# A four-stage software pipeline of a patch transformer, regrouped: normalization one round ahead, second norm with attention, and one late activation in the last layer

## The reference

```python
x = _fold_to_kernels(in_x)                      # (pixels, 3 tokens, 48)
h = _ln(x); q, k, v = split(h @ w_attn.T)       # 4 heads of 12
att = softmax(einsum('nhtd,nhsd->nhts', q, k) / sqrt(12))
x = x + einsum('nhts,nhsd->nhtd', att, v) @ w_attn_proj.T
h = _ln(x); x = x + gelu(h @ w_fc.T) @ w_fc_proj.T      # 48 -> 192 -> 48
x = _ln(x); out = einsum('bhwc,oc->bohw', sum(x, tokens), conv_w) + conv_b
```

## Time and profile before

| | us |
|---|---|
| median of 3 runs | 11524.5 (11506.01 to 11528.91) |
| the profiled execution | 11512.45 |
| its span | 11510.3 |
| PE busy | 8808.3 (77%) |
| DVE busy | 7862.0 (68%) |
| ACT busy | 7497.3 (65%) |
| POOL busy | 6400.2 (56%) |

### The profile page before, as it was taken

One profiled execution on the slowest core, in us unless ns is written; L12 is line 12 of the kernel. 1 busy time (PEld: TensorE's weight loads), 2 busy tenths in 40 slices (PEclk: granted clock), 3 DMA queues, 4 the chain that ended last, 5 costly groups with the idle time before them and its releaser, 6 DMA issues. The chain is left out here.

```text
span 11510.3 us, 144669 instructions
## 1 busy us (share of the span) xinstructions
PE 8808.3 (77%) x35038; PEld 2895.7 (25%) x35038; DVE 7862.0 (68%) x9543; ACT 7497.3 (65%) x8343; POOL 6400.2 (56%) x3353
## 2 busy tenths in 40 slices
PE   5888888888888888844008888888888888885588
PEld 2333323333333333311002222222222222221133
DVE  5555565555556555643748888888888888886677
ACT  3555555555555555523419889889889988985577
POOL 3444444444444444420008888888888888885111
PEclk8888888888888888877559999999999999998799
DMA  2000000000000000010432322233223322234554
GB/s 74 9 9 7 8 9 9 7 9 9 9 7 9 9 7 9 4 62 29 141 106 60 67 62 59 60 68 65 60 60 67 67 60 60 65 66 91 138 126 117
DMA packets 284359, 562.90 MB, mean 49 GB/s; under 512 B 75120, under 2 KB 205904, under 8 KB 270172
## 3 DMA queue, kind: packets, MB, share of 16 engines
q1 hardware_dynamic: 247858, 536.71, 19.5%
q0 software_dynamic: 35744, 17.87, 0.8%
HBM read 367.98 MB, written 186.07 MB: 48 GB/s over the span
## 5 line engine op out<-in xcount | busy, mean ns | idle before, releaser
L1188 POOL TENSOR_TENSOR l_a<-l_a 128x1018 f32<-128x1018 f32 x2116 | 3920.9, 1883 | 600.4 <-ACT l_a L1349 587.4
L1311 DVE TENSOR_TENSOR l_r<-l_pps,l_a 128x509 f32<-128x509 f32 x4232 | 2642.3, 680 | 651.7 <-PE l_pps L1201 651.6
L1349 ACT ACTIVATE l_a<-l_a 128x2036 f32<-128x2036 f32 x1193 | 2270.1, 1903 | 126.4 <-DVE l_a L1317 100.5
L1201 PE MATMUL l_qps<-l_mv,l_wst 123*128 123x509 bf16 x4246 | 1318.7, 393 | 889.0 <-DMA l_mv<-pw 567.5
L1342 ACT ACTIVATE l_a<-l_qps 128x1018 f32<-128x1018 f32 x1592 | 1591.6, 1019 | 471.9 <-PE l_qps L1201 457.1
L586 POOL TENSOR_TENSOR a_pr<-a_pr 128x768 f32<-128x768 f32 x384 | 877.1, 2284 | 1248.2 <-DVE a_pr L529 1232.4
L540 DVE TENSOR_TENSOR a_x<-a_cps,a_x 128x512 f32<-128x512 f32 x384 | 260.8, 688 | 1624.2 <-PE a_cps L417 1142.8
L665 ACT ACTIVATE a_g<-a_fps 128x512 f32<-128x512 f32 x1152 | 646.0, 595 | 1110.7 <-PE a_fps L410 848.5
L1201 PE MATMUL l_pps<-l_mv,l_wst 123*128 123x509 bf16 x4232 | 1342.9, 389 | 10.9 <-DVE l_r L1311 5.0
L1254 PE MATMUL l_aux<-l_r,l_sums 128*32 128x509 f32 x8448 | 1129.4, 607 | 54.3 <-DVE l_o L1295 33.3
L463 POOL TENSOR_TENSOR a_pr<-a_qkv 128x768 f32<-128x768 f32 x128 | 344.3, 2707 | 1256.5 <-ACT a_qkv L671 1256.5
(11 more groups left out here) (178 smaller groups left out, 11989.3 us busy)
## 6 DMA issues: line engine op xcount, KB each, us to landing
l_mv<-pw SPq DMA_DIRECT2D x1608, 79.5 KB
l_gx<-g SPq DMA_DIRECT2D x66, 1040.0 KB
planes<-l_s SPq DMA_DIRECT2D x67, 1018.0 KB, 4.6
l_sh<-planes SPq DMA_DIRECT2D x536, 127.2 KB, 6.5
a_xt<-g SPq DMA_DIRECT2D x192, 160.0 KB, 3.3
pw<-pw_hi SPq DMA_DIRECT2D x165, 127.2 KB
...
```

The costliest lines, as they stand in the source:

```text
L1188: g.tensor_tensor(a, a, a, ALU.mult).then_inc(sq_p, 1)
L1201: return t.matmul(out, wst[:, k, n * P:(n + 1) * P], x[:, n // NPP, cols], start=True, stop=True)
L1311: v.tensor_tensor(to, pps[:, (2 * m + h) % P_BANKS, 0:SUB], pair_of(A, m)[:, h, :], ALU.mult).then_inc(mul_done, 1)
L1349: s_.activation(a, a, ACT.Abs_reciprocal_sqrt, bias=1.0).then_inc(root_done, GROUP)
```

## The change

In the first layer the steps are regrouped. `STAGE` is now "ahead" (chunk n: centre, var1, `scale_tokens`), "new" (chunk n-1: heads, products, scores, softmax shift and `Exp`), "attn" (chunk n-2: values, mix, project, and now also `square_residual`, `var2` and `scale_residual`), "mlp" (chunk n-3: hidden, gelu, shrink, `add_mlp`, and now also `square_out`, `var3`, `scale_out`, `add_out` and the store). There are still 67 rounds. `Tc` gets a fourth slot, `QKV` a second one, the input `XT` has two slots instead of three. Within a round the groups of the mlp come first, then `project` alternating with `centre` and `var1`, then `var2`, then `var3`. In the last layer each `silu` comes one unit later.

```diff
-TURNS = 3
+TURNS = 4
+SLOTS0 = 2
 BANK = 512
 
-T_GROUPS = {"centre": (3, "new"), "var2": (6, "mlp"), "var1": (3, "new"), "var3": (6, "out"), "mix": (6, "attn")}
+T_GROUPS = {"mix": (6, "attn"), "centre": (3, "ahead"), "var1": (3, "ahead"), "var2": (6, "attn"), "var3": (6, "mlp")}
 C_GROUPS = {"mlp": (6, "mlp"), "proj": (6, "attn")}
-STAGE = {"new": 0, "attn": 1, "mlp": 2, "out": 3}
+STAGE = {"ahead": 0, "new": 1, "attn": 2, "mlp": 3}
+MIX_AT = {3: (0, 1), 4: (2, 3), 5: (4, 5)}
...
+        XT = sb("a_xt", [F2, SLOTS0, TW * H])
         Tc = sb("a_tc", [P, TURNS, TW * H])
...
-        QKV = sb("a_qkv", [P, TW, 3 * F2])
+        QKV = sb("a_qkv", [P, 2, TW, 3 * F2])
...
-                    if n + TURNS < NCHUNKS:
+                    if n + SLOTS0 < NCHUNKS:
                         sp.wait_ge(t_made, p.t_base + p.t_at["centre"] + 3)
-                        load(n + TURNS)
...
-                        pe.wait_ge(h1_made, p.n * 3 + 3)
-                    pe.wait_ge(q_read, p.n * TW + w + 1)
+                        pe.wait_ge(h1_made, p.n * 3)
+                    pe.wait_ge(q_read, (p.n - 1) * TW + w + 1)
...
                 def body(p):
-                    if p.new:
-                        pe.wait_ge(x_in[p.turn], (p.n - p.turn) * 16 + 48)
-                        for g in range(3):
-                            centre(p, g)
-                    if p.mlp:
-                        for g in range(6):
-                            var2(p, g)
-                        hidden(p, 0)
-                    if p.new:
-                        for g in range(3):
-                            var1(p, g)
-                    if p.out:
-                        for g in range(6):
-                            var3(p, g)
                     for g in range(7):
-                        if p.mlp and 0 < g < 6:
+                        if p.mlp and g < 6:
                             hidden(p, g)
                         if p.mlp and g:
                             shrink(p, g - 1)
                         if p.mlp and g < 6:
                             hidden_rest(p, g)
-                        if p.new and 0 < g < 6:
-                            heads(p, 2 * g - 2)
-                            heads(p, 2 * g - 1)
-                        if p.attn and g:
-                            mix(p, g - 1)
+                        if p.new and g < 5:
+                            heads(p, 2 * g)
+                            heads(p, 2 * g + 1)
+                        if p.attn:
+                            for q in MIX_AT.get(g, ()):
+                                mix(p, q)
+                    if p.ahead:
+                        pe.wait_ge(x_in[p.turn % SLOTS0], (p.n - p.turn % SLOTS0) * 24 + 48)
+                    for g in range(6):
+                        if p.attn:
+                            project(p, g)
+                        if p.ahead:
+                            (centre if g < 3 else var1)(p, g % 3)
                     if p.attn:
                         for g in range(6):
-                            project(p, g)
+                            var2(p, g)
+                    if p.mlp:
+                        for g in range(6):
+                            var3(p, g)
...
                     if p.attn:
                         softmax_scale(p)
                         values(p, 0)
                     if p.mlp:
+                        add_mlp(p, 0)
+                    if p.attn:
+                        values(p, 1)
+                    if p.mlp:
+                        add_mlp(p, 1)
+                    if p.attn:
+                        values(p, 2)
+                    if p.mlp:
+                        for g in range(2, 6):
+                            add_mlp(p, g)
+                    for g in range(6):
+                        if p.attn:
+                            add_attention(p, g)
+                        if p.new and g in (1, 2, 3):
+                            products(p, g - 2)
+                    if p.new:
+                        for n in range(5):
+                            score(p, n)
+                        softmax_shift(p)
+                    if p.attn:
                         for g in range(6):
                             scale_residual(p, g)
-                    if p.attn:
-                        values(p, 1)
-                        values(p, 2)
-                    if p.mlp:
-                        for g in range(5):
-                            add_mlp(p, g)
-                    if p.new:
-                        products(p)
-                    if p.mlp:
-                        add_mlp(p, 5)
-                    for g in range(6):
-                        if p.new and g < 5:
-                            score(p, g)
-                        if p.attn:
-                            add_attention(p, g)
-                    if p.new:
-                        softmax_shift(p)
 
                 steps(dve, body)
 
             @block.gpsimd
             def _(pool):
                 g_ = nc.gpsimd
+                pool.sem_inc(z_made, 3)
 
                 def add_values(p, d):
...
 
                 def body(p):
                     if p.attn:
-                        add_values(p, 0)
+                        for d in range(3):
+                            add_values(p, d)
                     if p.new:
+                        pool.wait_ge(q_read, p.n * TW + 2)
+                        if p.attn:
+                            pool.wait_ge(val_p, (p.n - 1) * 6)
+                        for d in (-2, 2):
+                            query_key(g_, p, d).then_inc(sc_p, 1)
+                    if p.ahead:
                         for g in range(3):
                             scale_tokens(p, g)
-                    if p.attn:
-                        add_values(p, 1)
-                        add_values(p, 2)
-                    if p.out:
+                    if p.mlp:
                         for d in range(3):
                             scale_out(p, d)
-                    if p.new:
-                        pool.wait_ge(q_read, p.n * TW + TW + 2)
-                        if p.attn:
-                            pool.wait_ge(val_p, p.n * 6)
-                        for d in (-2, 2):
-                            query_key(g_, d).then_inc(sc_p, 1)
-                    if p.out:
                         add_out(p)
...
                 def read_mix(p, g):
                     s_.activation(yT[:, g, :], made(p, "mix", g)[0:F2, :], ACT.Copy).then_inc(t_read, 1)
 
                 def body(p):
-                    if p.new:
+                    for g in range(6):
+                        if p.mlp:
+                            gelu(p, g)
+                        if p.new and g < 5:
+                            read_heads(p, 2 * g)
+                            read_heads(p, 2 * g + 1)
+                        if p.attn:
+                            for q in MIX_AT.get(g, ()):
+                                read_mix(p, q)
+                        if p.mlp and g in (3, 5):
+                            square_out(p, g // 4)
+                    if p.ahead:
                         for g in range(3):
                             read_centre(p, g)
                     if p.mlp:
+                        square_out(p, 2)
+                    if p.ahead:
+                        for g, (w, n) in enumerate(CENTRE):
+                            inverse_std(p, "var1", g, R1[:, w * H:(w + n) * H])
+                    if p.attn:
                         for d in range(3):
                             square_residual(p, d)
-                    if p.attn:
-                        act.wait_ge(soft, (p.n - 1) * 9 + 6)
-                        s_.activation(At[:], At[:], ACT.Exp, scale=float(HEAD) ** -0.5).then_inc(soft_exp, 1)
-                    if p.mlp:
                         for g in range(6):
                             inverse_std(p, "var2", g, R2[:, g, :])
-                    if p.new:
-                        for g, (w, n) in enumerate(CENTRE):
-                            inverse_std(p, "var1", g, R1[:, w * H:(w + n) * H])
-                    if p.out:
+                    if p.mlp:
                         act.wait_ge(stored, (p.n - 3) * (SETS * 16) + 16)
                         for g in range(6):
                             inverse_std(p, "var3", g, R3[:, g // 2, g % 2 * BANK:(g % 2 + 1) * BANK])
-                    for g in range(7):
-                        if p.mlp and g < 6:
-                            gelu(p, g)
-                        if p.new and 0 < g < 6:
-                            read_heads(p, 2 * g - 2)
-                            read_heads(p, 2 * g - 1)
-                        if p.attn and g:
-                            read_mix(p, g - 1)
-                    if p.mlp:
-                        for d in range(3):
-                            square_out(p, d)
+                    if p.new:
...
             def silu_after(n):
 
```

(2 more changed lines are left out.)

83 lines of the change are left out of this document (41 added, 42 removed).

## The result

| | before | after |
|---|---|---|
| median of 4 runs, us | 11518.5 | 10478.2 (10454.3 to 10487.8) |
| profiled execution, its span, us | 11512.45, 11510.3 | 10485.04, 10483.2 |
| granted clock over the span | 0.877 | 0.922 |

The ratio is 0.909, with a 95% interval of 0.9075 to 0.9113.

The account below looks back on a forecast made before the run. No engine is full, so the order of waits decides. A round of 38.3 + 29.8 = 68.1 us instead of 77.36 saves 565, the last layer 45: 11512.45 - 565 - 45 = 10902.5, median 10915 us, range 10610 to 11290.

Parts of the forecast that it names:

- part B: From the end of the last shrink to the next round's first Gelu: 29.8 us forecast instead of 40.8.
- the clock term: Ahead of var2, TensorE idles about 1.9 us and its clock falls: 1.5 us added, between 0 and 5.
- the first stretch of part A: From a round's first Gelu to the third Gelu of group 1: 11.0 us plus 1.3 for two heads.
- The charge of 1.3 for two heads at half clock: Group 0 gets two heads while TensorE is the slower partner: 1.3 us added, between 0 and 2.
- rival 1: Smaller gain, about 11280 us: GpSimd runs beside VectorE, products cost 6.33 us, half clock follows, round 73.8; chance 0.27.
- the tail: Two mixes and the last shrink, after the third Gelu of group 5: 3.6 us instead of 3.2.
- The first and last rounds: Three rounds at each end of the first layer, same work in other portions: 0 us, bounds 30 either way.
- groups 1 to 4 of part A: Between first Gelu and last shrink: groups 1 and 2 taken as 5.1 us each, groups 3 and 4 as 6.1.
- the three products: VectorE's products, after GpSimd has done its own: 3.2 us for three instead of 6.33.
- the pause of 3.62 us: TensorE waits ahead of hidden_rest(0) for the first Gelu: 3.7 us forecast where there were 2.69.
- the silu: Last layer: one unit later gives loads more time; 45 us saved, up to 105, later gathers possibly losing 20.
- Rival 2: Larger gain, about 10540 us: fewer pauses keep the clock full in early groups and var2, round 61.8; chance 0.10.

Follow-up runs that it names:

- n1: The kernel after, with project, centre and var1 one after the other instead of in turn; 10893.0 us, ratio to before 0.946.
- h1: The kernel after, with each pair of heads one group later (groups 1 to 5 instead of 0 to 4); 10627.4 us, ratio to before 0.922.
- f1: The kernel before, with four unread matmuls of 128 columns in the gap behind hidden_rest(0); 11374.1 us, ratio 0.988.
- h2: h1 with four unread matmuls of 128 columns in the gap behind hidden_rest(0); 10564.8 us, ratio to before 0.917.
- n3: n1 with six unread matmuls of 128 columns in the pause ahead of var2; 10821.2 us, ratio to before 0.939.
- f3: The kernel before, with seven unread matmuls of 128 columns in its pause of 1.77 us ahead of var2; 11516.9 us, ratio 1.000.
- f2: The kernel after, with 14 unread matmuls of 128 columns right behind hidden(0), in the pause before the first Gelu; 10419.9 us, ratio to before 0.9048.

## Why the prediction was wrong

- **The mechanism of part B was right.** A round lost its pauses there, and the engines follow each other as described. From the end of the last shrink (2036.2) the first inverse root starts after 7.9 us, the three squares end after 13.0 (forecast 13.1), the twelve roots after 24.4 (25.0), and the Gelu comes after 27.7, where 28.3 was the sum without the clock term. n1 shows what that order carries: 415 us, of which its own part is 4.7 us a round.
- **The failed step is the first stretch of part A**, "11.0 + 1.3" = 12.3 us. It took 8.6. Three things make up the 3.7 us. The base was wrong by 0.9: 11.0 is the longest of three kinds of round, and the mean was 10.1. The charge of 1.3 for two heads at half clock did not come. And the stretch got 1.5 shorter than before, where the forecast kept the half clock as long as it was, since the pause ahead of it is no shorter. h1, f1 and h2 show that the half clock's length hangs on the small gap behind the pause as well: work put there takes 1.6, 1.6 and 1.2 us off the stretch, even work nobody reads. So the heads were not a cost of 1.3 us but a gain of 1.6. Over 61 full rounds the 3.7 us are 226 us of the 437 missing.
- **The clock term of var2**, 1.5 us, failed next: 92 us. The pause was 1.51 us instead of 1.9, TensorE had run without a gap since 2003.15, and the clock stayed at 1.00 in all 59 rounds. By n3 a fall would have cost 1.4 us in part B, so the size was right and the fall did not come. Why not is shown in part only: in n1, where another pause of 1.51 us stands just before, it falls in 54 of 59 rounds. That "in every round of now a half clock follows a pause", which spoke for rival 1, holds for the first stretch and not for var2: its first four matmuls ran at full clock in 20 of 59 rounds before. By f3 the half clock there cost nothing in the kernel before.
- **Small terms**: the tail 2.9 us instead of 3.6, part B apart from the clock 0.5 us shorter: 1.2 x 61, 73 us. With the two above this is 391 us. The first and last rounds, taken at 0, gave 23 us more (987 for the layer, 15.8 x 61 = 964 for full rounds). What is left of the 437 is no larger than the spread of the layers that were not changed.
- **Right by size**: groups 1 to 4 of part A (5.15, 5.15, 6.0, 6.0 against 5.1 and 6.1), the three products (3.24 against 3.2), the pace of 1.99 us for two inverse roots, the pause of 3.62 us (3.7), and the silu (43 and 36 us by medians against 45; part of the wait moved to `gather`, which had been named only as a loss).
- **Wrong without effect**: `scale_residual`, 9.06 us in the sum, took 3.70. VectorE waits 5.5 us for `Exp` behind it.
- **Rival 2** came closest, in part by luck: a round of 61.8 against 61.6 measured (its own terms, 5 and 1.5 us off 68.1, give 61.6), 10540 against 10478 us. var2 ran at full clock as it said. The first stretch did not: TensorE was at half clock for some 3 us of it, and it took 8.6 us, not the 7.3 that 5 us less would make. The tail and part B made up the rest, which rival 2 had not named. It had 0.10 because its objection, the long pause, was true; the pause came, and did not decide. f2 reaches a stretch of 7.0 and a round of 59.9 us by filling the pause too.
